# Expert outputs scattered by token and rank, plain loads to combine them, rows gathered two groups ahead

## What is computed

```
scores = jax.nn.softmax(x @ w_router.T, axis=-1)
topw, topi = jax.lax.top_k(scores, K)                 # E, K = 64, 6
combine = zeros(T, E).at[arange(T)[:, None], topi].add(topw)
def body(acc, ws):
    g, v, o, cw = ws
    return (acc + cw[:, None] * _swiglu(x, g, v, o), None)
routed, _ = jax.lax.scan(body, zeros_like(x), (wg, wv, wo, combine.T))
...
x = _layernorm(x + _L0_ffn_ref(x, ...), axis=-1)      # routed + shared expert
x = _layernorm(x + _L1_attn_ref(x, ...), axis=-1)
```

## Time and profile before

| | us |
|---|---|
| median of 3 runs | 1000.24 (993.2 to 1004.77) |
| profiled execution | 987.55 |
| its span, first to last instruction | 985.7 |
| PE, DVE, ACT, POOL busy | 870.2, 720.6, 510.4, 407.1 |
| DMA moved in the span | 106.46 MB |

### The profile page before, as it was taken

One profiled execution on the slowest core, in us unless ns is written; L12 is line 12 of the kernel. 1 busy time (PEld: TensorE's weight loads), 2 busy tenths in 40 slices (PEclk: granted clock), 3 DMA queues, 4 the chain that ended last, 5 costly groups with the idle time before them and its releaser, 6 DMA issues.

```text
span 985.7 us, 15418 instructions
## 1 busy us (share of the span) xinstructions
PE 870.2 (88%) x5267; PEld 568.3 (58%) x5271; DVE 720.6 (73%) x1377; ACT 510.4 (52%) x1022; POOL 407.1 (41%) x338
## 2 busy tenths in 40 slices
PE   7999999999999999988889999999546867899886
PEld 3466666666565666656666777677423654343443
DVE  5667786959696867768774556665467798998797
ACT  3563554545544444445444334455522457898485
POOL 0203448494848577534214333333377312221013
PEclk9999999999999999989999999999866998999998
DMA  5451212112131221100926999999633000000001
GB/s 189 153 196 27 65 49 86 70 65 77 58 102 53 81 75 65 44 1 1 238 94 216 298 311 310 313 312 303 179 96 98 26 1 3 5 8 6 1 6 38
DMA packets 54743, 106.46 MB, mean 108 GB/s; under 512 B 8909, under 2 KB 26645, under 8 KB 54165
## 3 DMA queue, kind: packets, MB, share of 16 engines
q1 hardware_dynamic: 48917, 89.88, 29.6%
q0 software_dynamic: 5760, 15.74, 6.0%
HBM read 88.45 MB, written 17.14 MB: 107 GB/s over the span
## 4 chain that ended last, share of the span: by engine, by line
PE 54%; DVE 19%; DMA 10%; issue 5%; ACT 5%; SPq 3%; POOL 3%; DVEq 0%; ACTq 0%; POOLq 0%
PE ps L777 10%; PE ps L715 6%; DMA w_dn<-in_w_dn 5%; PE ps L873 5%; PE ps L725 4%; DVE row_max L2696 3%; PE ps L948 3%; DMA y_dram<-y_out 3%; PE ps L1280 3%; POOL key_part L1507 2%; DVE state L2119 2%; PE ps L795 2%; PE ps L960 2%; DMA key_part<-y_dram,slot_idx 2%; PE ps L1266 2%
## 5 line engine op out<-in xcount | busy, mean ns | idle before, releaser
L1479 POOL DMA_INDIRECT xg<-x_dram,tok_of x68 | 65.1, 958 | 131.8 <-PE ps L1006 94.2
L777 PE MATMUL ps<-w_vg,xT 128*128 128x512 f32 x256 | 116.8, 597 | 1.2 <-DVE th L2162 1.2
L1429 POOL TENSOR_TENSOR state<-state,rows_bc 128x1024 f32<-128x1024 f32 x22 | 53.8, 2446 | 95.5 <-DVE state L2119 41.9
L715 PE MATMUL ps<-xT,w_qks 128*128 128x512 f32 x192 | 86.5, 596 | 5.2 <-ACT qT L1585 5.2
L948 PE MATMUL ps<-w_gv,xgT 128*128 128x352 f32 (+1 forms) x272 | 87.4, 464 | 2.5 <-DMA w_dn<-in_w_dn 2.4
L2696 DVE TENSOR_REDUCE row_max<-ps 128x4 f32<-128x1024 f32 x64 | 74.3, 1217 | 7.1 <-PE ps L1245 6.3
L2130 DVE TENSOR_TENSOR aT<-ps,tri 128x768 f32<-128x768 f32 x64 | 59.7, 954 | 27.0 <-PE ps L725 26.9
L1585 ACT ACTIVATE probT<-ps 128x512 f32<-128x512 f32 x128 | 69.5, 594 | 10.1 <-PE ps L1266 9.6
L777 PEld LDWEIGHTS ps<-w_vg,xT 128*128 128x128 f32 x256 | 45.8, 190 | 48.8 <-issue 43.1
L960 PE MATMUL ps<-w_dn,hidT 88*128 88x256 f32 (+1 forms) x272 | 70.0, 379 | 0.0
L948 PEld LDWEIGHTS ps<-w_gv,xgT 128*128 128x128 f32 x272 | 48.9, 190 | 27.0 <-issue 5.2
(11 more groups left out here) (327 smaller groups left out, 2066.6 us busy)
## 6 DMA issues: line engine op xcount, KB each, us to landing
w_gv<-in_w_gv SPq DMA_DIRECT2D x68, 352.0 KB, 8.2
rows_bc<-x_dbl_dram SPq DMA_DIRECT2D x32, 512.0 KB, 3.8
w_dn<-in_w_dn SPq DMA_DIRECT2D x68, 192.0 KB, 9.6
y_dram<-y_out SPq DMA_DIRECT2D x68, 128.0 KB, 7.5
y_dram<-blank SPq DMA_DIRECT2D x4, 1408.0 KB, 13.2
w_vg<-in_wvg SPq DMA_DIRECT2D x8, 512.0 KB, 4.9
w_qks<-in_wqks SPq DMA_DIRECT2D x8, 384.0 KB, 3.1
w_o<-in_wo SPq DMA_DIRECT2D x8, 256.0 KB, 2.7
```

Of the source, the lines that this page charges most:

```text
L715: last = mm(bank(PJ + n % 2), w_qks[:, k, part * P:(part + 1) * P], xT[:, k, half * 512:(half + 1) * 512], start=(k == 0), stop=(k == KD - 1))
L777: last = mm(bank(PJ + t % 2), xT[:, k, t * P:(t + 1) * P], w_vg[:, k, :], start=(k == 0), stop=(k == KD - 1))
L1429: G.tensor_tensor(state_of(m), state_of(m), c_row[:, n % 2], ALU.mult).then_inc(read_out, 1)
L1479: G.indirect_dma_start(xg[:, j, :], None, x_dram, bass.IndirectOffsetOnAxis(ap=col, axis=0)).then_inc(gathered[j], 16)
```

## The change

1. **Where outputs go.** `y_dram` is laid out by token and rank: 8 rows (`RANKS`) for each token, and behind them 1,024 spare rows. The block's 128 rows are scattered by POOL with an indirect DMA whose index column is `row_of`, instead of stored by SP. Unused slots go to spare rows. The fill with zeros at 39 us and `slot_idx` are gone.
2. **Codes.** ACT scales `blk_hot` by 8 x token + rank (`tok_code`), which needs one instruction for each of the 6 ranks instead of one for a tile. DVE makes `tok_of` out of the code with four instructions where one was, and `row_of` with two more. Two constants, `tok_code` and `spare`, are loaded.
3. **Two buffers.** `y_out` and `xg` have two halves. The DVE copy of group i waits for the scatter of group i - 2 (in the fixed groups), and rows are gathered two groups ahead. In the loop with run-time bounds both fall back to one half.
4. **Combine.** SP loads the 6 rows of a token tile in two plain DMAs of 384 KB (3 rows, 3 KB for each token), 16 in all, through a ring of four buffers.

```diff
+RANKS = 8
+CHUNK = TOPK // 2
-        y_out = sb("y_out", [P, NJ, D])
+        y_out = sb("y_out", [P, 2, NJ, D])
-        xg = sb("xg", [P, NJ, D])
+        xg = sb("xg", [P, 2, NJ, D])
-        y_dram = nc.dram_tensor("y_dram", (NBLK * P, D), F32).ap()
+        y_dram = nc.dram_tensor("y_dram", (RANKS * TOK + 2 * NJ * P, D), F32).ap()
@@ SP
-            for n in range(4):
-                dst = y_dram[(E + NJ) * P + n * free:(E + NJ) * P + (n + 1) * free, :]
-                sp.dma_start(dst.rearrange("(n p) d -> p n d", p=P),
-                             blank[:].unsqueeze(1).to_broadcast([P, free // P, D])).then_inc(y_blank, 16)
...
-                        store_y(d * RING + r, j)
+                        sp.wait_ge(down_copied, at(d * RING + r, NJ, j + 1) + TILES)
...
-            for r in range(RING):
-                for j in range(NJ):
-                    store_y(used - RING + r, j)
             sp.wait_ge(stacked, 6)
             for dst, src in ((f_in, "f_in"), (f_out[:], "f_out")):
                 sp.dma_start(dst, a[src]).then_inc(layer_loaded, 16)
+            for j in range(NJ):
+                sp.wait_ge(y_stored[j], at(used, 16, 0))
+                sp.sem_inc(load_due, 1)
+            by_token = y_dram[0:RANKS * TOK, :].rearrange("(q e) d -> q (e d)", e=RANKS)
+            for c in range(2 * TILES):
+                if c >= 4:
+                    sp.wait_ge(combined, B + CHUNK * (c - 3))
+                first = (1 + CHUNK * (c % 2)) * D
+                sp.dma_start(yg[:, c % 4, :], by_token[c // 2 * P:(c // 2 + 1) * P, first:first + CHUNK * D]
+                             ).then_inc(back[c % 4], 16)
@@ PE
-                if k == 0:
-                    pe.wait_ge(hot_scaled, t + 1)
+                pe.wait_ge(hot_scaled, n + 1)
@@ POOL
+            for i in range(2):
+                for j in range(NJ):
+                    if i:
+                        pool.wait_ge(gathered[j], 16)
+                    gather(i, j, tok_of[:, NJ * i + j:NJ * i + j + 1])
             for i in range(FIXED):
                 for j in range(NJ):
-                    pool.wait_ge(xg_turned, NJ * i + j + 1)
-                    gather(j, tok_of[:, NJ * (i + 1) + j:NJ * (i + 1) + j + 1])
+                    if i < FIXED - 1:
+                        pool.wait_ge(xg_turned, NJ * i + j + 1)
+                        pool.wait_ge(gathered[j], 16 * (i + 2))
+                        gather(i % 2, j, tok_of[:, NJ * (i + 2) + j:NJ * (i + 2) + j + 1])
...
+                    if i:
+                        pool.wait_ge(down_copied, NJ * (i - 1) + j + 1 + TILES)
+                        if i > 1:
+                            pool.wait_ge(y_stored[j], 16 * (i - 1))
+                        scatter(i % 2, j, row_of[:, NJ * (i - 1) + j:NJ * (i - 1) + j + 1])
             used = used_groups(pool)
             with pool.Fori(FIXED, used) as i:
                 for j in range(NJ):
                     pool.wait_ge(gathered[j], at(i, 16, 16))
...
+                    pool.wait_ge(y_stored[j], at(i, 16, -16))
...
-            for n in range(TILES * TOPK):
-                if n >= 8:
-                    pool.wait_ge(combined, B + n - 7)
-                G.indirect_dma_start(yg[:, n % 8, :], None, y_dram,
...
+                pool.wait_ge(down_copied, at(used, NJ, j + 1 - NJ + TILES))
+                pool.sem_inc(gather_due, 1)
+                scatter(0, j, row_last[:, j:j + 1])
@@ ACT
-                f(blk_hot[:, t % 2], blk_hot[:, t % 2], ACT.Copy, scale=tok_id[:, t:t + 1]).then_inc(hot_scaled, 1)
+                for k in range(TOPK):
+                    f(blk_hot[:, t % 2, k, :], blk_hot[:, t % 2, k, :], ACT.Copy, scale=tok_code[:, t, k:k + 1]
+                      ).then_inc(hot_scaled, 1)
@@ DVE
-            then(V.tensor_copy(slot_idx[:], slot[:]))
-            V.tensor_copy(tok_of[:], ps[:, Y + 1, 0:COLS]).then_inc(route_vec, 1)
+            V.tensor_copy(code_f, ps[:, Y + 1, 0:COLS])
+            then(V.tensor_scalar(tok_f, ps[:, Y + 1, 0:COLS], -0.5 * (TOPK + 1), 1.0 / RANKS, ALU.add, ALU.mult))
+            then(V.tensor_scalar(tok_f, tok_f, ROUND, None, ALU.add))
+            V.tensor_scalar(tok_of[:], tok_f, -ROUND, None, ALU.add).then_inc(route_vec, 1)
...
-                    if not first:
+                    if half is None:
                         dve.wait_ge(y_stored[j], at(i, 16, 0))
+                    elif i > 1:
+                        dve.wait_ge(y_stored[j], at(i, 16, -16))
```

More of the change, by code:

```diff
@@ L307, in build @@
         tok_cur = sb("tok_cur", [P, NJ], U32)
+        tok_code = sb("tok_code", [P, TILES, TOPK])
+        spare = sb("spare", [P, COLS])
+        row_of = sb("row_of", [P, COLS], U32)
+        row_cur = sb("row_cur", [P, NJ], U32)
+        row_last = sb("row_last", [P, NJ], U32)
         pick = sb("pick", [P, TOPK, E])
@@ L489, in build @@
         down_copied = sem("down_copied")
-        y_blank = sem("y_blank")
-        back = [sem(f"back{j}") for j in range(8)]
+        rows_placed = sem("rows_placed")
+        row_picked = sem("row_picked")
+        last_picked = sem("last_picked")
+        back = [sem(f"back{j}") for j in range(4)]
         combined = sem("combined")
@@ L934, in _ @@
             turn_x(1)
[L936 removed]
+            pe.wait_ge(moe_consts, 96)
             for t in range(TILES):
@@ L1001, in _, with turn_g, group @@
             shared_down(range(NJ, TILES))
-            def turn_g(i, j):
+            def turn_g(i, j, half):
                 pe.wait_ge(gathered[j], at(i, 16, 16))
                 for k in range(KD):
-                    last = nc.tensor.transpose(ps[:, 2 * j, k * P:(k + 1) * P], xg[:, j, k * P:(k + 1) * P], ident[:])
+                    last = nc.tensor.transpose(ps[:, 2 * j, k * P:(k + 1) * P], xg[:, half, j, k * P:(k + 1) * P], ident[:])
                 last.then_inc(xg_turned, 1)
-            def group(i, gv, dn):
+            def group(i, half, gv, dn):
                 def up_g(j):
@@ L1024, in group @@
                     down(i * NJ + (j + TILES), j, 2 * j + 1, lambda f: dn(j, f))
-                    turn_g(i + 1, j)
+                    turn_g(i + 1, j, half)
                     if j + 2 < NJ:
@@ L2416, in _ @@
             V.tensor_scalar(groups[:, 0:1], groups_f[:], float(FIXED), None, ALU.add).then_inc(route_vec, 1)
+            then(V.scalar_tensor_tensor(out=spare[:], in0=code_f, scalar=0.0, in1=spare[:], op0=ALU.is_equal, op1=ALU.mult))
+            V.tensor_tensor(row_of[:], code_f, spare[:], ALU.add).then_inc(rows_placed, 1)
             def rotate(src, dst, prods, tiles, n, size):
@@ L2457, in stack, with group @@
                     last.then_inc(stacked, 1)
-            def group(i, first=False, side=None):
+            def group(i, half=None, side=None):
                 for j in range(NJ):
```

90 lines of the change are left out of this document (48 added, 42 removed).

## The result

The changed kernel is slower. Its median is 1052.5 us (1041.7 to 1053.8, four runs) against 998.0 (993.2 to 1004.8) of the kernel before: a ratio of 1.052, with a 95% interval of 1.042 to 1.061. I had forecast 985.5 us and a range up to 1001. The profiled execution took 1051.6 us, with a span of 1049.8 against 985.7.

What follows compares the result with a forecast made beforehand. DMA throughput was taken to bound the loop and POOL's gather issue the combine. Terms -13.2 (combine), -1.2 (seam), +0.6 (bytes) and -0.8 (routing) gave -14.6 us: 972.9 profiled, 985.5 us on the median, range 974 to 1001.

Steps and rivals of the forecast that it cites:

- The loop: POOL: POOL's issue in the group loop: eight indirect DMAs fit under the pace, scatter 0.95 us, limit 1.06, no cost.
- rival 1: Loop: POOL becomes the bound and the kernel slower, up to 1027 us; chance 0.08 over 1%, 0.08 within 1%.
- slower by over 1%: Whole kernel: the outcome of losing more than 1%, from a scatter of about 1.47 us on; chance 0.08.
- Bytes: Loop's DMA traffic: -1.7 us for gathers moved earlier, +2.3 for outputs changing queue; sum +0.6, bounds -2 and +3.
- Rival 2: Loop: scattered rows cost the DMA engines more than gathers, loop 7.7 us longer, 992.5 us on the median; chance 0.14.
- rival 3: Loop becomes faster, down to PE's 10.0 us a group: -6 us, 979 us on the median; chance 0.14.
- Seam: From the last output copy to the first `add_row`: 6.5 + 2 - 9.7 = -1.2 us; bounds -3 and +1.
- Combine: Combine: plain SP loads remove 14.5 us of row waits, PE's projections add 1.3; net -13.2, bounds -15 and -12.
- rival 4: Combine gives back half: 7 us of waits return in place of 1.3, 991 us on the median; chance 0.13.
- Routing: Routing before the loop: scaling saves 2.0 us, `tok_of` adds 0.8, small loads 0.4; sum -0.8, bounds -2 and +1.
- Two groups ahead and the halves: Loop: four gathers (0.52 MB) move into the idle stretch at the start, saving 1.7 us.
- signs: Changed profile: no later `add_row` waits, combine about 49 us, higher PE clock, scatters 0.95 us, pace 10.3 to 10.6, DMA share over 1.

Runs made afterwards that it cites:

- e1: Changed kernel with outputs stored by SP block after block and no scatters, so POOL issues only four gathers a group: 984.1 us.
- e3: Changed kernel with its gathers replaced by plain loads of the same size on SP, the four scatters a group staying on POOL: 979.1 us.
- e8: Changed kernel with each scatter replaced by a plain store of the same 128 KB on POOL's queue, the four gathers staying: 978.7 us.
- e11: Changed kernel with POOL issuing a group's four gathers first and then its four scatters, instead of in turn: 1027.0 us.
- e4: Changed kernel with each scatter writing its 128 rows in order, block after block, instead of at places by token and rank: 1041.9 us.
- e6: Changed kernel with gathers for scatters, and those only for blocks 0 and 2, so POOL issues six indirect DMAs a group: 1025.2 us.
- e7: Changed kernel with a small memset on POOL behind every indirect DMA of the fixed groups: 1039.5 us.
- e10: Changed kernel with a fixed group's weights loaded by two DMAs of four blocks each in place of eight, same bytes: 1027.1 us.
- e16: Changed kernel with a group's scatters behind its gathers and the weights of two blocks in one load: 1026.8 us, ratio 1.022 to 1.036.
- e2: Changed kernel with each scatter replaced by a second gather of the same 128 KB, still eight indirect DMAs a group: 1057.7 us.
- e12: Kernel before with only the halves of `xg` and `y_out` and gathers two groups ahead: 986.3 us against 988.9, ratio 1.000.
- e14: Changed kernel with gathers for scatters, the second four of a group moving 64 rows instead of 128: 992.8 us, kernel before 988.9 there.
- e15: Changed kernel with four blocks' weights in one load and a group's scatters behind its gathers: 998.6 us, kernel before 988.9 there.

## Why the prediction was wrong

**The step that failed** is "The loop: POOL": "It issues 8 indirect DMAs of 1.25 us in a group, 10.0 of 10.46 us. Now it waits 93.9 us in the loop, which is the cover ... I take 0.95 for a scatter and no cost." The scatter's own time was nearly right (1.00 us, under the limit of 1.06), and POOL did not become the bound. But I took POOL's waiting as time in which an issue costs nobody anything. What had kept the other engines free was that its DMAs came only four in a row. With eight in a row 1.29 us apart, ACT, DVE and PE stand for 3 to 5 us at a time in most groups, and the loop pays 74 us. PE's lower clock has a part in that which no run separates. No rival of mine had this mechanism; rival 1 had the side and the place, but its price was POOL's own time, worth 41 us at 1.74 us for each scatter. All of "slower by over 1%" had a chance of 0.08.

**The rest of the sum came out near**, and the runs with four indirect DMAs show it: e1 took 984.1 us, e3 979.1 and e8 978.7, where the forecast was 985.5. Each leaves out something that the changed kernel does (e1 and e8 the scatters, e3 the gathers), and by term the sum was less good than its total.

- *Bytes:* forecast +0.6 us. The loops of e3 and e8, which move the same bytes with and without scatters, take 178.9 and 179.1 us against 177.9. Right in size as far as these runs go, since none has four gathers and four scatters without holds. Rival 2 (DMA engines pay for scatters) and rival 3 (a faster loop) find nothing for them in either. The Trainium skill, page "DMA: Bandwidth & Descriptors", section "Issuing engines are not separate DMA queues", agrees for the throughput: 308 GB/s (e3) and 317 (e8) with the outputs on POOL's queue, 316 (e1) on SP's.
- *Seam:* forecast -1.2, measured -1.8 us, which is luck in part. The term had 2 us for a last copy that waits for its buffer. In a loop slowed to 15 us a group that wait didn't come: DVE's last copy, from 777.09 to 777.51 us, waits for no DMA. The rest took 7.8 us instead of 6.5. POOL issues the last scatter 1.0 us after the copy, behind the three others, where I had 0.2; it lands in 3.09 us for 2.73, and the first load in 3.59 for 3.1. The chain of after:

```profile
778.54 3.09 DMA y_dram<-y_out,row_last
...
781.72 3.59 DMA key_part<-y_dram
```

- *Combine:* the step was right and its size off. The waits for rows went from 17.6 us to 1.0, as forecast. But DVE now waits 6.8 us for PE's projections, where I had allowed 1.1 + 1.3 on the ground that PE's clock would rise. It stayed where it was, 0.73 after 0.71. The 4.4 us more cover the 3.4 by which the term missed. This is rival 4 in part: of the 14.5 us, 4.7 came back, against 1.3 in the forecast and 7 in the rival. What I held against it, that PE idles for half of the stage, was misread: from 722.3 to 771.1 us it was busy 32.6 of 48.8 us, two thirds. Of after: waits from 780 to 840 us, the row on all `add_row`, and a window of the combine:

```profile
DVE lk L2562 <- PE ps L1092: 6.8, 6, 2.4
L2576 DVE SCALAR_TENSOR_TENSOR xres<-key_part,pick_w,xres x48: 466/484/486, 785.3 to 836.6; 128x256 f32<-128x256 f32 x48
796.40:811.30 14.90, 10.39 (x37) 6.31 (x37) 13.40 (x30) 4.83 (x13) 0.00 (x0) 0.73 0.35 106
```

- *Routing:* forecast -0.8 with +1 as its upper bound, measured +4.3. In after most of it is PE's clock. The router's 32 matmuls took 6.93 us in place of 3.89, at the lower level (granted 0.50, 1.2 GHz) from 474 to 482 us, where the kernel before had 0.93, after the same 3.2 us of idle time. Windows of after, then of e11, which has the same routing:

```profile
474.00:482.00 8.00, 8.00 (x39) 7.84 (x38) 0.31 (x3) 1.31 (x3) 0.68 (x4) 0.50 0.94 236
```
```profile
474.00:482.00 8.00, 6.84 (x44) 5.59 (x43) 4.17 (x28) 3.54 (x19) 1.76 (x8) 1.00 0.95 247
```

  The other runs show two more cases. In e11 the router took 3.68 us and group 0 began at 521.66 us, against 521.27 before. In e1 to e4, e6, e7, e10 and e16 the router took 3.7 to 4.0 us, but group 0 began at 523.2 to 523.9: PE waited 1.9 to 3.0 us for the shared expert's weights (0.7 before, 1.2 in e11), and the 16 matmuls behind that wait took 6.7 us in place of 5.0, at a granted clock of 0.75 in e2 and e3. Two small loads stand ahead of these weights now, a term that I had put at 0.4. So the change itself costs 0.4 us in the best case and 2 to 2.6 us where that wait is long, and the rest in after is the router at half clock. From the scores to `tok_of` the path grew by 0.7 us (32.5 to 33.2); I had expected it 1.2 shorter (-2.0 + 0.8).
- *Two groups ahead and the halves:* forecast a part of -1.7 us, measured nothing (e12: 1.000).

In what I had listed as signs, the first came true (no wait of `add_row` behind the first), the second nearly (51.8 us in place of 49), and the scatters too (1.00 us, 1.29 apart, for 0.95 and 1.25). PE's clock in the combine did not rise. "The pace of a group 10.3 to 10.6 us" and "the DMA share still over 1" were the ones that showed the error.

**What stays open** is the mechanism. The rows show SP's issues and the starts of ACT and DVE held together, so I think of a path that their signals share with what POOL sends for an indirect DMA; no run shows that path. Two stretches don't fit a plain count: in the kernel before, POOL issues 48 gathers 1.25 us apart in the combine, and after them twelve in a row ahead of group 1 in the changed kernel, and neither stretch has waits of this kind on the scale of the loop. The combine has none on ACT and DVE. Beside the twelve and just behind them ACT has some of 1.0 to 1.8 us, and group 0 took 15.7 us there, against 10.1 before and 12.3 in e12, so that stretch isn't free either. Why one chip hardly shows the holds is open as well; e14 and e15 were run there once each.

## What to carry to other kernels

An engine's waiting time is not room for more DMA issues at no cost. On POOL, a fifth to eighth indirect DMA in a row, 1.2 to 1.3 us apart beside a busy pipeline of PE, ACT and DVE, held the others up by some 5 us a group, while four in a row, or six at 1.9 us, hardly held them (six at 1.9 us made POOL's own time the limit). Before a stage gets more indirect DMAs, count how many POOL will issue without a break, and where they can't be spaced, leave the transfer with SP as a plain one. In a trace, look for waits that end with nothing the profile can name, and for two DMA issues with no wait between them that are further apart than elsewhere.

## What the hardware showed that I had not expected

- Indirect DMAs on POOL delay other engines' starts and SP's issues whatever their direction (1057.7 us with gathers only), their addresses (1041.9 in order), the load beside them (1039.9 with small weights) or their rows (1065.4 with half as many in every second one). What helps is distance: six in a group at 1.25 us cost 1025.2 us, at 1.9 us 996.9.
- One chip differed in it by far more than in speed: the same kernel took 992.8 us on it (one run) and 1065.4 on another, while the kernel before took 988.9 and 997.3.
- A small POOL instruction between two indirect DMAs is free: a memset of 0.17 us moved the next one by 0.03 us. Two that wait for each other moved it by 0.6 us or more (starts 1.87 to 2.00 us apart for 1.25).
